# One exponential for two like score blocks, and TensorE's sums placed by steps of scores, in an attention kernel

## Chip, cores and metric

One Trainium2 chip, one core. The metric is the device time of the whole kernel in microseconds (us). PE is TensorE, ACT is ScalarE, DVE is VectorE, POOL is GpSimd, SP is the engine that issues the DMAs.

## What is computed

The input `x` has 2048 rows of 128 numbers, all float32. The reference is four residual blocks one after the other:

```
x = x + attention_a(layernorm(x))     # 16 heads of 8, causal, bias slope_h * (k - q)
x = x + ffn(layernorm(x))             # token shift, sigmoid gate, squared relu
x = x + attention_b(layernorm(x))     # linear attention with rotary positions
x = x + ffn(layernorm(x))
```

Only the softmax attention of the first block is touched by the change. For each head, `attn = Q K^T / sqrt(8) + bias`, with -inf where the key lies behind the query, then a softmax over the keys and a product with `V`.

## The kernel before

The heads are handled in transposed form: a block of scores has 128 keys on the partitions and up to 512 queries in the free dimension. The 2048 queries are four chunks `c` of 512, the 16 heads four groups `g` of 4, and a group is two pairs `u` of two heads `v`. The two heads of a pair sit on the two halves of TensorE's rows (64 each, `SIDE`), so their two score products run side by side, into two neighbouring banks of PSUM.

A block `(kb, w0, w1)` is key tile `kb` against the columns `w0` to `w1` of the chunk: the columns that the causal mask leaves, and only as far as the bias lets a head reach (`live`). A pair of heads has a list of blocks for a chunk (`pair_blocks`): blocks on the diagonal, which are 512, 384, 256 and 128 columns wide, take turns with blocks before it, which are mostly 512 wide. For the heads with steep slopes (g = 0, and pair 0 of g = 1) the blocks away from the diagonal are shorter and fewer, so one pair can have a block where the other has none.

A *unit* is the i-th block of both pairs of a group, 152 units in all, listed in `plan` in the order `ORDER` of (c, g). A *step* is what one exponential handles: before, one block of one pair, both heads, so up to 2 x 512 = 1024 columns; a unit has one or two steps, 296 in all.

- TensorE computes the scores of step n into the banks 2 * (n % 3) and the next one (`score`, the matmul is L1139). It waits for `exp_done`, until the exponential of step n - 3 is finished.
- ScalarE computes one exponential a step from PSUM into a slot in SBUF (`exps`, L532). There are four slots, used in turn by units: the first exponential of unit n also waits for `pv_done`, until the sums of unit n - 4 are done.
- VectorE masks the diagonal square of the units on the diagonal (`follow`, L856), and when a group has ended turns the sums (L790) and divides (`scale`).
- TensorE multiplies the probabilities with the values (`weigh`, the matmul is L1168): four matmuls for the four heads of a unit (eight records in the trace), which write four groups of 32 partitions and run side by side. They accumulate over the units of a group in bank 6 or 7 (`lane`). `weigh` waits for the unit's exponentials and its mask.

The order on TensorE is written out: while unit m is at hand, it issues the scores of pair 0 of unit m + 2, then `weigh` of unit m - 1, then the scores of pair 1 of unit m + 2. In the groups of chunk 3 some `aside`s of the next block (output projection, transposes of the second layernorm) stand behind that. After the last unit of `plan` the remaining sums are done and the rest of the kernel follows (72 us), which the change leaves alone.

The rows of queries and keys (`qr`, `kr`) are written by DMAs which SP issues from 9 to 115 us. SP also loads `x` again, once the sums of the last unit that used it as a slot are done.

Of the kernel before, what the change touches and what calls it, by code (L numbers as in the profile page):

```python
# [15 lines left out]
ACT = mybir.ActivationFunctionType  # L16
AX = mybir.AxisListType

P = 128
# [5 lines left out]
CH = 512  # L25
NCH = T // CH
TPC = CH // P
# [10 lines left out]
SIDE = 64  # L38
# [25 lines left out]
def program(nc, x_in, w_in, c_in, cb_in, krow_in, qrow_in, out):  # L64
    with ExitStack() as ctx:
        def sb(name, shape, dt):
            return ctx.enter_context(nc.sbuf_tensor(name, shape, dt))
# [4 lines left out]
        ps = ctx.enter_context(nc.psum_tensor("ps", [P, 8, CH], F32))  # L72
# [25 lines left out]
        summed = sb("summed", [P, 4 * TPC, V1], F32)  # L98
# [7 lines left out]
        with ExitStack() as rows:  # L106
# [3 lines left out]
            qr = [row_tensor(f"qr{n}") for n in range(NCH)]  # L110
            kr = [row_tensor(f"kr{n}") for n in range(NCH - 1)]
# [31 lines left out]
        def sems(names):  # L143
# [27 lines left out]
        s_done, exp_done, mask_done, pv_done, ot_ready, o_recip, o_norm = sems(  # L171
            "s_done exp_done mask_done pv_done ot_ready o_recip o_norm")
# [39 lines left out]
        def units_of(group, lane):  # L212
            c, g = group
            both = list(zip_longest(*(pair_blocks(c, 2 * g + u) for u in range(2))))
            return [(c, g, i, lane, i == len(both) - 1, blocks) for i, blocks in enumerate(both)]

        plan = []
        for k, group in enumerate(ORDER):
            units = units_of(group, k % 2)
            for c, g, i, lane, last, blocks in units:  # L220
                diagonal = all(b and b[0] >= TPC * c for b in blocks)
                steps_before, masks_before = (plan[-1].step + sum(b is not None for b in plan[-1].blocks),
                                              plan[-1].masks + plan[-1].masked) if plan else (0, 0)
                plan.append(Unit(c, g, i, lane, len(plan), last, blocks, diagonal, steps_before, masks_before))

        ends = [unit for unit in plan if unit.last]
# [6 lines left out]
        ASIDES = 3  # L233
        assert all(ends[k].i > i for k, i in ASIDE)
        assert all(b.n - a.n >= SCALE for a, b in zip(ends, ends[1:]))
        STEPS = plan[-1].step + sum(b is not None for b in plan[-1].blocks)

        def step_of(unit, u):
            return unit.step + (u if unit.blocks[0] else 0)

        def steps_with(unit):
            return unit.step + sum(b is not None for b in unit.blocks)


        def in_x(unit):
# [232 lines left out]
        def _(act):  # L478
# [37 lines left out]
            def exps(unit):  # L516
                slot = probs_slot(unit)
                act.wait_ge(pv_done, unit.n + 1)
                if unit.n == 3:

                    act.wait_ge(v_psum, NCH)
                if unit.n == min(other.n for other in plan if other.n % 4 == 1 and not in_x(other)):
                    for m in range(2):
                        for g in range(G):
                            act.wait_ge(rows_loaded[NCH - 1][m][g], ROW_LOADS[NCH - 1])
                for u, block in enumerate(unit.blocks):
                    if block:
                        _, w0, w1 = block
                        n = step_of(unit, u)
                        act.wait_ge(s_done, n + 1)  # L530
                        b = 2 * (n % 3)
                        nc.scalar.activation(slot[:, 2 * u:2 * u + 2, w0:w1], ps[:, b:b + 2, w0:w1], ACT.Exp).then_inc(exp_done, 1)  # L532
# [452 lines left out]
        def _(pe):  # L985
# [143 lines left out]
            def score(unit, u):  # L1129
                if unit is None or unit.blocks[u] is None:  # L1130
                    return
                kb, w0, w1 = unit.blocks[u]
                n = step_of(unit, u)
                wait_rows(unit.c, 0, unit.g)
                wait_rows(kb // TPC, 1, unit.g)
                pe.wait_ge(exp_done, n + 1)
                for v in range(2):
                    a, j = SIDE * v, 2 * unit.g + u
                    ins = nc.tensor.matmul(ps[:, 2 * (n % 3) + v, w0:w1],  # L1139
                                           kr[kb // TPC][a:a + SIDE, j, P * (kb % TPC):P * (kb % TPC + 1)],  # L1140
                                           qr[unit.c][a:a + SIDE, j, w0:w1], start=True, stop=True)
                ins.then_inc(s_done, 1)


# [5 lines left out]
            def weigh(unit):  # L1150
                if unit.i == 0:

                    ended = [place[e.c, e.g] for e in ends if e.lane == unit.lane and e.n < unit.n]
                    if ended:
                        pe.wait_ge(ot_ready, 1 + max(ended))
                    if place[unit.c, unit.g] == 1:

                        pe.wait_ge(v_ready[0], 2)
                        pe.wait_ge(v_ready[1], 2)
                    wait_asides(place[unit.c, unit.g] - 1)  # L1160
                pe.wait_ge(exp_done, 3 + steps_with(unit))
                if unit.masked:
                    pe.wait_ge(mask_done, unit.masks + 1)
                for v in range(4):
                    if unit.blocks[v // 2]:
                        kb, w0, w1 = unit.blocks[v // 2]
                        h = 4 * unit.g + v
                        ins = nc.tensor.matmul(ps[32 * v:32 * v + V1, 6 + unit.lane, w0:w1], vaug[:, kb, V1 * h:V1 * (h + 1)],  # L1168
                                               probs_slot(unit)[:, v, w0:w1],
                                               start=(unit.i == 0), stop=unit.last, skip_group_check=True)  # L1170
                ins.then_inc(pv_done, 1)
# [99 lines left out]
            def usual_path():  # L1271
                rows_seen.clear()
                pe.wait_ge(v_ready[0], 1)
                pe.wait_ge(v_ready[1], 1)
                nc.tensor.matmul(ps[:, 1, 0:2 * P], cb[:, B_ID:B_ID + P], cb[:, 0:2 * P], start=True, stop=True).then_inc(branched, 1)
                for u in range(2):
                    score(plan[0], u)

                pe.wait_ge(parts_ready, 2 * NCH)
                values(2)  # L1280
                for u in range(2):
                    score(plan[1], u)
                values(3)

                for unit, ahead in zip_longest(plan, plan[2:]):
                    score(ahead, 0)
                    if unit.n:
                        weigh(plan[unit.n - 1])
                    score(ahead, 1)
                    aside(unit)  # L1290
                weigh(plan[-1])

                mix_k_in(0, 0)
                mix_r_in(0, 0)
                project(3)
                mix_out(0, 0)
                mix_k_in(0, 1)
                mix_r_in(0, 1)
                mix_k_in(0, 2)
                mix_out(0, 1)  # L1300
                mix_r_in(0, 2)
                turn_ln2(3)
                mix_out(0, 2)
                mix_k_in(0, 3)
                turn_ln3(0)
                mix_r_in(0, 3)
                turn_ln3(1)
                mix_out(0, 3)
                k_b(0)
                v_b(0)  # L1310
                turn_ln3(2)
                k_b(1)
                q_b(0)
                v_b(1)
                k_b(2)
                turn_ln3(3)
                q_b(1)
                k_b(3)
                summarize(0)
                v_b(2)  # L1320
                v_b(3)
                q_b(2)
                summarize(1)
                q_b(3)
                summarize(2)
                summarize(3)
                turn_q(0)
                turn_q(1)
                numerators(0)
                turn_q(2)  # L1330
                numerators(1)
                turn_heads(0)
                numerators(2)
                project_b(0)
                turn_q(3)
                turn_heads(1)
                numerators(3)
                turn_heads(2)
                project_b(1)
                project_b(2)  # L1340
                turn_heads(3)
                turn_ln4(0)
                project_b(3)
                mix_k_in(1, 0)
                turn_ln4(1)
                mix_r_in(1, 0)
                turn_ln4(2)
                mix_k_in(1, 1)
                mix_r_in(1, 1)
                turn_ln4(3)  # L1350
                mix_k_in(1, 2)
                mix_r_in(1, 2)
                mix_out(1, 0)
                mix_out(1, 1)
                mix_k_in(1, 3)
                mix_out(1, 2)
                mix_r_in(1, 3)
                mix_out(1, 3)
# [72 lines left out]
```

## Time and profile before

| | us |
|---|---|
| Time of three runs, median (lowest to highest) | 333.89 (333.45 to 337.83) |
| The profiled execution: its own time | 333.41 |
| The profiled execution: span in the trace | 331.6 |
| TensorE busy in the span | 302.4 (91%) |
| ScalarE busy | 286.5 (86%) |
| VectorE busy | 162.2 (49%) |
| Mean granted clock of TensorE | 0.998 of full |

The first of the 296 exponentials begins at 24.2 us, the last ends at 259.4, and the last sum ends at 260.5; the attention of the first block is this stretch. A row of a timeline is a run of like instructions: its start, its length, the engine, the line, what is written from what, the shape of the first, how many. What stands in brackets is how long the engine was idle before it, and who ended that. Two instructions of one engine can overlap in such rows, since an instruction's record begins before the one ahead of it has drained; the cost of one in a stream is therefore read from the distance between two starts or two ends.

### The profile page before, as it was taken

The numbers are of one execution on the slowest core, as the hardware profiler recorded it, in microseconds if no ns is written. First come the engines' busy times: TensorE is split into PE (matmuls) and PEld (weight loads), VectorE is DVE, ScalarE is ACT, GpSimd is POOL, SyncE is SP. The second block draws the span as 40 slices with busy tenths as digits, with TensorE's granted clock in tenths as the row PEclk, the third lists the DMA queues.
The fourth block names the chain that finished last, engine by engine and source line by source line (L and its number), as shares of the span: only waits on it lengthen the run. The fifth ranks groups of instructions, "written<-read, shape, count | busy, mean of one in ns | idle before, by whom it ended". The sixth has DMA issues, their size and how long they took to land.

```text
span 331.6 us, 6146 instructions
## 1 busy us (share of the span) xinstructions
PE 302.4 (91%) x2306; PEld 131.1 (40%) x2306; DVE 162.2 (49%) x426; ACT 286.5 (86%) x410; POOL 57.5 (17%) x56
## 2 busy tenths in 40 slices
PE   2977999999999999999999999999999998979784
PEld 1633232333333222232323323333232567878563
DVE  6853243276633040311351461353713396999885
ACT  8548999989999999999899999998999488963782
POOL 5897000000040000000000110100000052811540
PEclk9999999999999999999999999999999999999999
DMA  7444443444464400000030000000000000000004
GB/s 212 118 114 98 103 140 96 104 110 88 108 199 104 103 2 0 2 0 2 0 112 17 2 1 2 0 2 0 2 1 2 0 3 0 3 0 2 0 0 131
DMA packets 14291, 16.45 MB, mean 50 GB/s; under 512 B 2513, under 2 KB 9041, under 8 KB 14161
## 3 DMA queue, kind: packets, MB, share of 16 engines
q1 hardware_dynamic: 14256, 16.01, 18.7%
q8 instruction: 20, 0.33, 0.4%
q14 instruction: 15, 0.11, 0.1%
HBM read 6.56 MB, written 2.62 MB: 28 GB/s over the span
## 4 chain that ended last, share of the span: by engine, by line
ACT 34%; PE 32%; DVE 16%; issue 13%; DMA 2%; POOL 1%; SPq 1%; DVEq 0%; ACTq 0%
ACT probs L532 23%; PE ps L1168 14%; PE ps L1139 10%; ACT x L532 8%; PE ps L993 4%; DVE stats L657 2%; ACT parts_last L532 2%; PE ps L1006 2%; DVE scr L916 2%; DMA x<-in_x 2%; DVE scr L905 1%; ACT scr L541 1%; POOL rstd L424 1%; DVE x L891 1%; DVE scr L930 1%
## 5 line engine op out<-in xcount | busy, mean ns | idle before, releaser
L532 ACT ACTIVATE probs<-ps 128x1024 f32<-128x1024 f32 (+5 forms) x223 | 169.0, 860 | 9.2 <-PE ps L1139 8.1
L1139 PE MATMUL ps<-qr,kr 64*128 64x512 f32 (+6 forms) x592 | 108.6, 420 | 7.2 <-ACT probs L532 4.2
L1168 PE MATMUL ps<-probs,vaug 128*9 128x512 f32 (+5 forms) x892 | 97.5, 495 | 1.1 <-DVE probs L856 1.1
L1139 PEld LDWEIGHTS ps<-qr,kr 64*128 64x128 f32 x592 | 49.3, 184 | 122.6 <-ACT probs L532 80.2
L856 DVE TENSOR_TENSOR probs<-probs,cs 128x512 f32<-128x512 f32 x60 | 41.3, 689 | 97.3 <-ACT probs L532 97.1
L424 POOL TENSOR_TENSOR rstd<-veps,neghalf 128x4 f32<-128x4 f32 x16 | 17.1, 1066 | 194.5 <-DVE veps L663 194.5
L532 ACT ACTIVATE x<-ps 128x1024 f32<-128x1024 f32 (+6 forms) x47 | 41.7, 950 | 0.1
L993 PE MATMUL ps<-w,scr 128*128 128x128 f32 x288 | 37.1, 280 | 2.6 <-DVE scr L877 1.1
L993 PEld LDWEIGHTS ps<-w,scr 128*128 128x128 f32 x288 | 34.4, 192 | 7.9 <-DVE scr L877 2.4
L532 ACT ACTIVATE parts_last<-ps 128x1024 f32<-128x1024 f32 (+5 forms) x26 | 24.1, 965 | 2.7 <-PE ps L1139 2.5
L1168 PEld LDWEIGHTS ps<-probs,vaug 128*9 128x9 f32 x892 | 13.7, 89 | 28.4 <-issue 16.4
L1168 PE MATMUL ps<-x,vaug 128*9 128x512 f32 (+6 forms) x188 | 22.8, 536 | 0.0
L790 DVE STREAM_TRANSPOSE ot<-ps 128x512 f32<-128x512 f32 x16 | 11.5, 717 | 16.7 <-PE ps L1168 16.4
L541 ACT ACTIVATE scr<-x,shift_by,rstd 128x128 f32<-128x128 f32 x36 | 14.8, 483 | 5.0 <-POOL shift_by L429 4.9
L988 PE MATMUL ps<-cs,scr 128*128 128x128 f32 x80 | 12.4, 280 | 2.6 <-ACT scr L541 2.1
L657 DVE BATCH_NORM_STATS2 stats<-x 128x6 f32<-128x128 f32 x64 | 13.9, 280 | 1.6 <-DMA x<-in_x 1.2
L488 ACT COPY scr<-ps 128x512 f32<-128x512 f32 x17 | 9.7, 579 | 5.8 <-PE ps L988 5.6
L453 POOL MEMSET kr<- 128x4096 f32 x1 | 3.5, 3514 | 61.1 <-DMA kr<-parts_mid 61.1
L1168 PE MATMUL ps<-parts_last,vaug 128*9 128x512 f32 (+5 forms) x104 | 13.9, 555 | 0.0
L988 PEld LDWEIGHTS ps<-cs,scr 128*128 128x128 f32 x80 | 8.8, 141 | 6.1 <-ACT scr L541 4.4
L815 DVE TENSOR_TENSOR x<-ps,x 128x512 f32<-128x512 f32 x4 | 2.8, 692 | 16.2 <-PE ps L993 16.2
L448 POOL MEMSET qr<- 128x4096 f32 x3 | 10.5, 3510 | 0.0
(106 smaller groups left out, 236.5 us busy)
## 6 DMA issues: line engine op xcount, KB each, us to landing
x<-in_x SPq DMA_DIRECT2D x8, 256.0 KB, 3.9
qr<-parts_mid SPq DMA_DIRECT2D x32, 64.0 KB, 2.5
kr<-parts_mid SPq DMA_DIRECT2D x32, 64.0 KB, 2.5
kr<-att SPq DMA_DIRECT2D x16, 64.0 KB, 2.4
qr<-att SPq DMA_DIRECT2D x16, 64.0 KB, 2.6
qr<-parts_last SPq DMA_DIRECT2D x16, 64.0 KB, 2.6
kr<-parts_last SPq DMA_DIRECT2D x16, 64.0 KB, 2.4
out_y<-x SPq DMA_DIRECT2D x4, 256.0 KB, 3.1
```

The costliest lines, as they stand in the source:

```text
L424: nc.gpsimd.tensor_tensor(rstd[:, n], veps[:, n], neghalf[:], ALU.pow).then_inc(ln_rstd[l], 1)
L448: nc.gpsimd.memset(z.bitcast(F32)[:, :, :], 0.0).then_inc(zeroed, 1)
L488: nc.scalar.copy(dst, ps[:, bank, :]).then_inc(ready, 1)
L532: nc.scalar.activation(slot[:, 2 * u:2 * u + 2, w0:w1], ps[:, b:b + 2, w0:w1], ACT.Exp).then_inc(exp_done, 1)
L541: ins = nc.scalar.activation(xh[:, P * t:P * (t + 1)], x[:, t, :], ACT.Identity, bias=shift_by[:, n, j:j + 1], scale=rstd[:, n, j:j + 1])
L657: nc.vector.bn_stats(stats[:, n, j, :], x[:, TPC * n + j, :]).then_inc(dve_step, 1)
L790: nc.vector.transpose(ot[:], ps[:, 6 + ends[k].lane, :]).then_inc(ot_ready, 1)
L856: nc.vector.tensor_tensor(slot, slot, cs[:, C_TRI:C_TRI + P].unsqueeze(1).broadcast_to([P, 4, P]), ALU.min).then_inc(mask_done, 1)
L988: ins = nc.tensor.transpose(ps[:, bank, P * j:P * (j + 1)], src[:, P * j:P * (j + 1)], ident)
L993: ins = nc.tensor.matmul(ps[:, bank, P * j:P * (j + 1)], src[:, P * j:P * (j + 1)], w[:, c0:c0 + D], start=True, stop=True)
L1139: ins = nc.tensor.matmul(ps[:, 2 * (n % 3) + v, w0:w1], kr[kb // TPC][a:a + SIDE, j, P * (kb % TPC):P * (kb % TPC + 1)], qr[unit.c][a:a + ...
L1168: ins = nc.tensor.matmul(ps[32 * v:32 * v + V1, 6 + unit.lane, w0:w1], vaug[:, kb, V1 * h:V1 * (h + 1)], probs_slot(unit)[:, v, w0:w1], st ...
```

## The change

Where both pairs of a unit have the same block and it is at most 256 columns wide, the unit is now one step: TensorE writes four score products, pair 0 into the columns from 0 and pair 1 into the columns from 256 of the same two banks, and ScalarE takes both with one exponential of four pieces (pair, head, columns) where there were two exponentials. `weigh` for such a unit is unchanged. The order on TensorE is no longer "pair 0, sum, pair 1" but goes by steps: the sum of unit n is issued right behind the scores of step `due[n]`, which is four steps after the unit's last one, or the first step of unit n + 4 if that comes sooner. The last four sums stand behind all scores.

```diff
+        def in_one(unit):
+            return unit.blocks[0] == unit.blocks[1] and unit.blocks[0][2] - unit.blocks[0][1] <= CH // 2
+
+        def steps_with(unit):
+            return unit.step + (1 if in_one(unit) else sum(b is not None for b in unit.blocks))
...
+        def has_step(unit, u):
+            return unit is not None and unit.blocks[u] is not None and not (u and in_one(unit))
 
         def step_of(unit, u):
-            return unit.step + (u if unit.blocks[0] else 0)
+            return unit.step + (u if unit.blocks[0] and not in_one(unit) else 0)
...
+                if in_one(unit):
+                    _, w0, w1 = unit.blocks[0]
+                    act.wait_ge(s_done, unit.step + 1)
+                    b = 2 * (unit.step % 3)
+                    nc.scalar.activation(slot[:, :, w0:w1].rearrange("p (u v) q -> p u v q", u=2),
+                                         ps[:, b:b + 2, :].rearrange("p v (u q) -> p u v q", u=2)[:, :, :, 0:w1 - w0],
+                                         ACT.Exp).then_inc(exp_done, 1)
+                    return
...
+                one = in_one(unit)
+                if one and u:
+                    return
...
-                for v in range(2):
-                    a, j = SIDE * v, 2 * unit.g + u
-                    ins = nc.tensor.matmul(ps[:, 2 * (n % 3) + v, w0:w1],
-                                           kr[kb // TPC][a:a + SIDE, j, P * (kb % TPC):P * (kb % TPC + 1)],
-                                           qr[unit.c][a:a + SIDE, j, w0:w1], start=True, stop=True)
+                for pair in range(2) if one else (u,):
+                    c0 = CH // 2 * pair if one else w0
+                    for v in range(2):
+                        a, j = SIDE * v, 2 * unit.g + pair
+                        ins = nc.tensor.matmul(ps[:, 2 * (n % 3) + v, c0:c0 + w1 - w0],
+                                               kr[kb // TPC][a:a + SIDE, j, P * (kb % TPC):P * (kb % TPC + 1)],
+                                               qr[unit.c][a:a + SIDE, j, w0:w1], start=True, stop=True)
...
+                due = [min(steps_with(unit) + 4, plan[unit.n + 4].step) for unit in plan[:-4]]
+                summed = 0
                 for unit, ahead in zip_longest(plan, plan[2:]):
-                    score(ahead, 0)
-                    if unit.n:
-                        weigh(plan[unit.n - 1])
-                    score(ahead, 1)
+                    for u in range(2):
+                        if has_step(ahead, u):
+                            score(ahead, u)
+                            while summed < len(due) and due[summed] <= step_of(ahead, u):
+                                weigh(plan[summed])
+                                summed += 1
                     aside(unit)
-                weigh(plan[-1])
+                for unit in plan[summed:]:
+                    weigh(unit)
```

Of the 152 units, 32 become one step: in each of the 16 groups the diagonal block of 256 columns and that of 128. The steps fall from 296 to 264.

## Rows read from the trace of the kernel before

**Rows 1.** The page: busy time by engine, its share of the span, instructions.

```profile
PE 302.4 (91%) x2306; PEld 131.1 (40%) x2306; DVE 162.2 (49%) x426; ACT 286.5 (86%) x410; POOL 57.5 (17%) x56
```

**Rows 2.** The page's costliest groups: busy, mean of one, idle before and its releaser.

```profile
L532 ACT ACTIVATE probs<-ps 128x1024 f32<-128x1024 f32 (+5 forms) x223 | 169.0, 860 | 9.2 <-PE ps L1139 8.1
...
L856 DVE TENSOR_TENSOR probs<-probs,cs 128x512 f32<-128x512 f32 x60 | 41.3, 689 | 97.3 <-ACT probs L532 97.1
...
L532 ACT ACTIVATE parts_last<-ps 128x1024 f32<-128x1024 f32 (+5 forms) x26 | 24.1, 965 | 2.7 <-PE ps L1139 2.5
```

**Rows 3.** Timeline of ACT, four stretches with one exponential each: two pairs of neighbours.

```profile
161.49 0.38 ACT L532 ACTIVATE probs<-ps 128x256 f32<-128x256 f32 x1
...
161.75 0.39 ACT L532 ACTIVATE probs<-ps 128x256 f32<-128x256 f32 x1
...
164.73 1.02 ACT L532 ACTIVATE x<-ps 128x1024 f32<-128x1024 f32 x1
...
165.63 1.03 ACT L532 ACTIVATE probs<-ps 128x1024 f32<-128x1024 f32 x1
```

**Rows 4.** Timeline of PE in chunk 2, around wide blocks (units 66 to 70).

```profile
127.00 0.73 PE L1139 MATMUL ps<-qr,kr 64*128 64x512 f32 x4
127.66 0.41 PE L1168 MATMUL ps<-probs,vaug 128*9 128x128 f32 x8
...
128.81 0.50 PE L1139 MATMUL ps<-qr,kr 64*128 64x512 f32 x2 [0.31 <-ACT probs L532]
129.24 1.05 PE L1168 MATMUL ps<-probs,vaug 128*9 128x512 f32 x8
130.22 0.93 PE L1139 MATMUL ps<-qr,kr 64*128 64x512 f32 x4
```

**Rows 5.** The chain that ended last, in order of time: first exponentials of groups (2, 2), (2, 3).

```profile
115.30 1.14 ACT probs L532
...
134.95 1.14 ACT probs L532
```

**Rows 6.** Timeline of ACT in the groups of chunk 0.

```profile
73.10 2.50 ACT L532 ACTIVATE probs<-ps 128x256 f32<-128x256 f32 x3 [0.40 <-PE ps L1139]
...
78.67 2.50 ACT L532 ACTIVATE probs<-ps 128x256 f32<-128x256 f32 x3 [0.40 <-PE ps L1139]
```

**Rows 7.** Timeline of PE in the same groups.

```profile
77.06 0.33 PE L1139 MATMUL ps<-qr,kr 64*128 64x128 f32 x2 [0.32 <-ACT x L532]
77.32 1.05 PE L1168 MATMUL ps<-probs,vaug 128*9 128x512 f32 x8
78.30 0.61 PE L1139 MATMUL ps<-qr,kr 64*128 64x128 f32 x4
```

**Rows 8.** Timeline of ACT in group (2, 0), units 86 to 92.

```profile
157.62 2.73 ACT L532 ACTIVATE probs<-ps 128x768 f32<-128x768 f32 x5 [0.48 <-PE ps L1139]
...
162.71 0.84 ACT L532 ACTIVATE probs<-ps 128x800 f32<-128x800 f32 x1 [0.57 <-PE ps L1139]
163.81 1.02 ACT L532 ACTIVATE probs<-ps 128x1024 f32<-128x1024 f32 x1 [0.26 <-PE ps L1139]
```

**Rows 9.** Timeline of PE in the same stretch.

```profile
162.54 0.73 PE L1168 MATMUL ps<-x,vaug 128*9 128x328 f32 x8
163.20 0.50 PE L1139 MATMUL ps<-qr,kr 64*128 64x512 f32 x2
```

**Rows 10.** Timeline of ACT at the end of group (3, 1), unit 109.

```profile
191.48 1.02 ACT L532 ACTIVATE parts_last<-ps 128x1024 f32<-128x1024 f32 x1 [0.95 <-PE ps L1139]
```

**Rows 11.** Timeline of PE at the end of the attention.

```profile
257.19 0.49 PE L1139 MATMUL ps<-qr,kr 64*128 64x512 f32 x2
...
258.48 2.02 PE L1168 MATMUL ps<-probs,vaug 128*9 128x512 f32 x16
```

**Rows 12.** Groups of ACT from 0 to 30 us: other patterns and the shortest activation.

```profile
L501 ACT COPY vaug<-ps 128x512 f32<-128x512 f32 x1 | 0.6, 587 | 0.3 <-PE ps L993 0.3
L481 ACT ACTIVATE warm<-neghalf 128x1 f32<-128x1 f32 x1 | 0.2, 202 | 0.0
```

More of the change, by code:

```diff
@@ L221, in program @@
                 diagonal = all(b and b[0] >= TPC * c for b in blocks)
-                steps_before, masks_before = (plan[-1].step + sum(b is not None for b in plan[-1].blocks),
-                                              plan[-1].masks + plan[-1].masked) if plan else (0, 0)
+                steps_before, masks_before = (steps_with(plan[-1]), plan[-1].masks + plan[-1].masked) if plan else (0, 0)
                 plan.append(Unit(c, g, i, lane, len(plan), last, blocks, diagonal, steps_before, masks_before))
@@ L235, in program @@
         assert all(b.n - a.n >= SCALE for a, b in zip(ends, ends[1:]))
-        STEPS = plan[-1].step + sum(b is not None for b in plan[-1].blocks)
+        STEPS = steps_with(plan[-1])
+        def has_step(unit, u):
+            return unit is not None and unit.blocks[u] is not None and not (u and in_one(unit))
         def step_of(unit, u):
-            return unit.step + (u if unit.blocks[0] else 0)
-        def steps_with(unit):
-            return unit.step + sum(b is not None for b in unit.blocks)
+            return unit.step + (u if unit.blocks[0] and not in_one(unit) else 0)
         def in_x(unit):
```

## Prediction

> **What bounds the kernel now.** I read the page first, then the list of groups, then the timelines of ScalarE and TensorE side by side. The page alone misleads. TensorE looks busier than ScalarE, 91% against 86% [rows 1]; but matmul records overlap, so I take costs from starts and ends.
>
> ScalarE: neighbouring exponentials of 256 columns end at 161.87 and 162.14 (start plus length), 0.27 apart; of 1024 at 165.75 and 166.66, 0.91 apart [rows 3]. The difference, 0.64 for 768 columns, is 0.833 ns a column, and 0.27 - 256 x 0.000833 leaves 0.06 us fixed. The other widths follow: 0.49 for 512, 0.70 for 768. So a full unit of two wide blocks costs ScalarE 1.82 us.
>
> TensorE: two score steps of 512 columns that need not wait take 0.66 together, 0.33 each; one that was waited for takes 0.43 (128.81 to 129.24); the sum of a full unit 0.98 (129.24 to 130.22), that of a 128-wide unit some 0.34 (a record of 0.41 less the 0.07 by which that of the wide sum, 1.05, overlaps what follows) [rows 4]. A full unit costs TensorE 1.64. With wide blocks ScalarE is the bound and TensorE has 0.18 a unit to catch up with. The 296 steps have 240,300 columns: 296 x 0.06 + 240,300 x 0.000833 = 218 us of work for ScalarE, in the 235 us from the first start to the last end. So about 17 us are ScalarE's idle time, and 12 of them stand in the list as idle before L532, 10.6 ended by the scores L1139 [rows 2]. The change can win the fixed part of 32 exponentials, and some of these 17.
>
> Where the idle time sits: at narrow blocks and at units of one block. In chunk 0 a group has blocks of 512, 384, 256 and 128, and the same three exponentials come back 5.57 us later (73.10, 78.67) [rows 6]. ScalarE's work in such a group is 2 x (0.91 + 0.70 + 0.49 + 0.27) = 4.74, so 0.83 are idle. TensorE's row says why: the first 128-wide score goes out at 77.06, then a whole sum of 0.98 stands ahead of the second, at 78.30 [rows 7], while ScalarE has only the last 512 columns and 0.27 of work in hand. In group (2, 0) units 91 and 92 have one block, and each score has a sum ahead of it (162.54, 0.66 before the score of unit 92 at 163.20) [rows 9]; ScalarE idles 0.57 and 0.26 there [rows 8]. Group (3, 0) repeats it. The largest, 0.95, is before unit 109, one block behind two sums and a projection [rows 10].
>
> **The change, part by part.**
>
> *One exponential for two.* 32 times 0.06 is 1.9 us less work for ScalarE; the columns stay. This pays only where ScalarE is the bound, so I count it inside the groups below. The Trainium skill ("ScalarE: Activation LUTs", section "What ACT_TABLE_LOAD costs") says that an activation has 186 ns fixed with immediate operands and that neighbours overlap by about 93 ns, which leaves 93 ns for each one dropped, 3.0 us by that page for 32, 1.1 more than by the rows. The measurement decides.
>
> *The new pattern.* The exponential reads four pieces across two banks and jumps back to the first bank once. No exponential before does that. The nearest row on the low side is the copy of values, which writes 64 pieces of 8 and takes 587 ns for 512 columns, as ordinary ones do [rows 12]: extra 0. On the high side a one-column activation takes 202 ns [rows 12]; if each return to the first bank cost that, 32 x 0.20 = 6.4 us. I take 0, since the copy is the nearest in kind.
>
> *Four score products in a step.* The same products and weight loads as two steps; one wait less. The sum of TensorE's work is the same. But both pairs must be written before ScalarE starts, so a 256-wide unit is ready 0.22 later than its first half was. It is hidden while ScalarE has a wide exponential in hand (0.91).
>
> *Sums by steps.* Between wide units `due` gives the old order. Around the merged units a sum comes up to one unit later. That adds a wait: take units 63 to 67. Now the scores of step 67.0 are issued when the exponential of 65.0 is done (time 0), the sum of unit 63 stands behind them, and the first exponential of unit 67 needs that sum's slot. It is ready at 0.05 + 0.43 + 1.05 for the whole sum + about 0.1 for the signal = 1.63; ScalarE has 0.91 (65.1) and 0.49 (66) to do and, since neighbours overlap by 0.1, could start at 1.3. So a gap of about 0.35 arises in each group at the unit after the 128-wide one. Behind it wait all later exponentials on ScalarE, and TensorE's scores three steps on.
>
> Group by group:
> - Eight groups with c and g at least 1 (all but (3, 1)). Before: the 24 steps of (2, 2) are 21,504 columns, 19.35 of work, and took 19.65 (115.30 to 134.95) [rows 5], so 0.30 are idle. After: work less 0.12, idle 0.35. Sum 0, within 0.1.
> - Four groups of chunk 0. Work 4.62. The second 128-wide score is no more behind a sum, so the gap of 0.57 goes; the new wait of 0.35 stays. 4.62 + 0.35 = 5.0 against 5.57: 4 x 0.55 = 2.2 us won. TensorE's own work there, 8 score products of pairs and 4 sums, is 4.6 (a score 0.33 at 512 columns and, as I estimate from the 77.06 row, 0.16 at 128; a sum 0.98 and 0.34), so it just keeps up; if it doesn't, this term halves.
> - Three groups with g = 0. The scores of the single blocks now come before the sums that stood ahead. I leave about 0.15 of each gap: 0.57 + 0.26 become 0.3 in (2, 0) and (3, 0), with 0.12 for the merges 0.65 each, and (1, 0) has one such unit, 0.5. The gap of 0.48 before unit 86 [rows 8] stays, no merged unit is near. Together 1.8 won.
> - Group (3, 1): 0.95 at unit 109 becomes 0.4; its narrow units had some 0.6 of gaps, and its sums there are of short blocks, so the new wait is hidden. With the merges 1.3 won.
> - The end. Before, the sum of unit 148 stood ahead of the last scores (257.19); three sums followed, and the last began when the last exponential was done [rows 11]. Now four stand behind: 0.43 + 3 x 0.98 = 3.4 after the last scores begin, against an exponential that is done 2.7 later at best (three of 0.91). The last sum is 0.6 late, and the rest of the kernel waits for it: 0.6 lost.
>
> *At nothing.* Masks: 0.69 each [rows 2], in chunk 0 four in a group, 2.8 of 5.0 us; sums come later than before, so masks have more time. Without that cover each would stand on the path with up to 0.7. The divisions at a group's end shift by at most a sum. SP's queue moves nothing: rows are loaded by its own order, and its reload of `x` waits for the sum of unit 93, which is as late after its exponential as before, with 10 us to its first use.
>
> Sum: -2.2 - 1.8 - 1.3 + 0.6 = -4.7. Against the profiled execution's 333.41 this gives 328.7; the median of the runs is 0.5 higher, 329.2. I say 329.0.
>
> **The rivals.**
>
> 1. *TensorE doesn't get its lead back* (the new wait repeats, the old gaps stay). For it: in chunk 0 TensorE's work (4.6) and ScalarE's (4.62) are equal, and each waited-for score costs 0.1 more. Against it: in wide stretches it regains 0.18 a unit. Chunk 0 gives 1.1 instead of 2.2, the g = 0 groups 0.9 instead of 1.8, and six groups lose 0.1 each: -4.7 + 1.1 + 0.9 + 0.6 = -2.1, 331.5.
> 2. *More of the idle time goes*: the slack that ScalarE's early narrow work used is kept, and the chain of small delays that feeds on itself (0.48 at unit 86, gaps by the asides in chunk 3) shortens as well. Half of the 17 us is the most that I can name at such places: -8, 325.5.
> 3. *Slower: the four-piece exponential is dear.* Place: the 32 merged steps. Price: two restarts of 0.13 to 0.20 each, 0.26 to 0.4 a step, 8 to 13 us against 4.7 won: 337 to 342. It decides from 0.15 us a step on. Against it stands the copy with 64 pieces.
> 4. *It does not do what it says*: if the 32 merged steps saved nothing fixed because the instruction is split inside into its pieces, 1.9 us fall away, of which about half counted: 330.
>
> **How the numbers follow.** Forecast 50%; rival 1, 20%; rival 2, 12%; rival 3, 6%; rival 4, 12%. The forecast's own spread is 1.5 us, from the 0.15 left at a gap (0 to 0.3, eleven places) and the new wait (0.2 to 0.5 in twelve groups). The range from 325.9 to 332.6 holds the forecast, rivals 1 and 4 and the half of 2; it leaves out rival 3 and some of 2 and 1, under 20%. About 2% is what a measurement of this kernel can tell from no change: 6.7 us, so faster means under 327.2. That is rival 2 and a tail of the forecast, 17%; slower over 340.6 is the dear half of rival 3, 4%; within 2%, 79%.
>
> **What would show it.** The profile after should have 264 exponentials; neighbours of the merged forms should end 0.49 (512 columns) and 0.91 (1024) after the one before. The three like exponentials of chunk 0 should return after 5.0. ScalarE's idle time at units 91, 92, 109 should be 0.4 or less, and a gap of about 0.35, ended by the sums L1168 and not by scores, should stand before the unit behind each 128-wide one. The last scores should be followed by four sums, and the last sum should end about 4.4 after them. The stretch behind should last 72 us as before. I am wrong if the merged exponentials take longer than their columns, if the masks L856 release sums, or if TensorE's waits for exponentials vanish in chunk 0, which would mean that it has become the bound.

## Result and the profile after

| | before | after |
|---|---|---|
| Time, median of six runs each, us | 334.61 (333.45 to 337.83) | 329.95 (329.03 to 332.01) |
| Ratio, with its 95% interval | | 0.9865 (0.9829 to 0.9901) |
| The profiled execution: time, span | 333.41, 331.6 | 330.01, 328.2 |
| First exponential begins, last sum ends | 24.2, 260.5 | 23.9, 255.8 |
| That stretch | 236.3 | 232.0 |
| Behind it, to the end | 71.1 | 72.4 |

The change makes the kernel 1.35% faster, 4.7 us by the medians. The forecast was 329.0, from a gain of 4.7 us on the profiled execution of before. Between the two profiled executions the difference is 3.4: the first exponential begins 0.3 earlier and the attention is 4.3 shorter, but the rest behind it took 1.3 longer, 1.0 of it in a stretch with a lower clock (last section).

The page after, busy time and costliest groups of ScalarE:

```profile
PE 302.3 (92%) x2306; PEld 133.7 (41%) x2306; DVE 161.7 (49%) x426; ACT 283.2 (86%) x378; POOL 57.6 (18%) x56
...
L546 ACT ACTIVATE probs<-ps 128x1024 f32<-128x1024 f32 (+5 forms) x159 | 141.6, 996 | 9.0 <-PE ps L1158 5.7
...
L536 ACT ACTIVATE probs<-ps 128x1024 f32<-128x1024 f32 (+1 forms) x32 | 27.6, 881 | 0.0
```

Against [rows 1] ScalarE has 32 instructions fewer and 3.3 us less busy time. Line 536 is the merged exponential, 32 of them, none of which waited. L546 is what L532 was. Its idle time before `probs` is nearly what it was in [rows 2], 9.0 against 9.2, but it has another owner. The waits of ScalarE in the trace of after (waiting line, releaser, us in total, times, longest):

```profile
ACT probs L546 <- PE ps L1158: 5.7, 10, 1.5
...
ACT probs L546 <- PE ps L1187: 2.6, 11, 0.4
```

Scores (L1158) release 5.7 us where they released 8.1 [rows 2]. New are 11 waits of up to 0.4 for sums (L1187), and two more ahead of `parts_last`: the slot of four units back.

Timelines of ScalarE and then of TensorE around units 64 to 67 of group (2, 2), after:

```profile
117.87 1.23 ACT L536 ACTIVATE probs<-ps 128x1024 f32<-128x1024 f32 x1
118.78 2.16 ACT L546 ACTIVATE x<-ps 128x1024 f32<-128x1024 f32 x2
120.58 0.84 ACT L536 ACTIVATE probs<-ps 128x512 f32<-128x512 f32 x1
121.61 1.94 ACT L546 ACTIVATE probs<-ps 128x1024 f32<-128x1024 f32 x2 [0.19 <-PE ps L1187]
```

```profile
119.47 0.44 PE L1158 MATMUL ps<-qr,kr 64*128 64x128 f32 x4
120.07 0.50 PE L1158 MATMUL ps<-qr,kr 64*128 64x512 f32 x2 [0.16 <-ACT x L546]
120.50 1.05 PE L1187 MATMUL ps<-probs,vaug 128*9 128x512 f32 x8
121.47 0.51 PE L1158 MATMUL ps<-qr,kr 64*128 64x512 f32 x2
```

This is the new wait as it was stepped out. The exponential of 65.0 ends and releases the scores of 67.0 at 120.07; 0.43 later the sum of unit 63 begins, takes 1.05 to its end at 121.55, and at 121.61 the first exponential of unit 67 can start. The one before it began at 120.58 and, with 512 columns, needed 0.48 to 0.49: the merged form ends at 121.42, the pair before it at 120.94. A stream would have gone on 0.1 before 121.42, so ScalarE lost about 0.3. The bracket says 0.19, since it counts from the end of a record.

The groups of chunk 0, ScalarE, after, to be compared with [rows 6]:

```profile
72.28 1.94 ACT L546 ACTIVATE probs<-ps 128x1024 f32<-128x1024 f32 x2 [0.28 <-PE ps L1187]
74.10 1.52 ACT L546 ACTIVATE x<-ps 128x768 f32<-128x768 f32 x2
75.48 1.55 ACT L536 ACTIVATE probs<-ps 128x1024 f32<-128x1024 f32 x2
77.31 1.03 ACT L546 ACTIVATE probs<-ps 128x1024 f32<-128x1024 f32 x1 [0.28 <-PE ps L1187]
```

The period was 5.57 and is 5.03. The gap in front of the second 128-wide exponential is gone, and the whole of what idles now is the wait for the sum. TensorE in the same groups, after, for [rows 7]:

```profile
70.17 1.06 PE L1158 MATMUL ps<-qr,kr 64*128 64x128 f32 x6
71.17 1.05 PE L1187 MATMUL ps<-probs,vaug 128*9 128x512 f32 x8
```

Its wait of 0.32 for an exponential no longer shows. A timeline prints idle time only from 0.15 on. The first row holds three pairs of scores, and the third pair, 512 columns of the next group, starts at 70.74, 0.13 after the pair ahead of it has ended.

Group (2, 0), ScalarE, after, for [rows 8]:

```profile
154.21 1.75 ACT L546 ACTIVATE probs<-ps 128x768 f32<-128x768 f32 x3 [0.48 <-PE ps L1158]
155.88 1.02 ACT L536 ACTIVATE probs<-ps 128x1024 f32<-128x1024 f32 x1
156.80 1.23 ACT L546 ACTIVATE x<-ps 128x656 f32<-128x656 f32 x2
157.90 0.62 ACT L536 ACTIVATE probs<-ps 128x512 f32<-128x512 f32 x1
158.54 1.99 ACT L546 ACTIVATE probs<-ps 128x800 f32<-128x800 f32 x2
```

The idle 0.57 and 0.26 before units 91 and 92 no longer show; the 0.48 before unit 86 stands as it stood. Group (3, 1), ScalarE, after, where [rows 10] had 0.95:

```profile
165.89 0.81 ACT L546 ACTIVATE probs<-ps 128x768 f32<-128x768 f32 x1 [0.47 <-PE ps L1158]
...
171.49 0.87 ACT L546 ACTIVATE parts_last<-ps 128x832 f32<-128x832 f32 x1 [0.23 <-PE ps L1187]
...
186.53 1.03 ACT L546 ACTIVATE parts_last<-ps 128x1024 f32<-128x1024 f32 x1
187.94 1.94 ACT L546 ACTIVATE probs<-ps 128x1024 f32<-128x1024 f32 x2 [0.38 <-PE ps L1158]
```

Unit 109 (186.53) comes without a gap, but 0.38 of it has moved to the unit behind, 0.23 stands in front of unit 101 for a sum, and 0.47 before the second exponential of unit 96.

The end of the attention, TensorE, after, for [rows 11]:

```profile
251.78 0.50 PE L1158 MATMUL ps<-qr,kr 64*128 64x512 f32 x2 [0.42 <-ACT probs L546]
252.21 1.05 PE L1187 MATMUL ps<-probs,vaug 128*9 128x512 f32 x8
253.07 1.04 PE L1187 MATMUL ps<-parts_last,vaug 128*9 128x512 f32 x8
253.93 1.90 PE L1187 MATMUL ps<-probs,vaug 128*9 128x512 f32 x16
```

Four sums behind the last scores. They start 0.86 apart, not 0.98: a sum that follows a sum needs 0.12 less than one with a score behind it.

### The profile page after: what moved, and what is told of

It is laid out like the page before. It is cut to its first block, busy times and chain, and to the rows that moved or that the text cites. A ratio compares the mean times of both kernels' runs of the same rounds, so it can differ in the third digit from the quotient of the medians.

```text
span 328.2 us, 6114 instructions
## 1 busy us (share of the span) xinstructions
PE 302.3 (92%) x2306; PEld 133.7 (41%) x2306; DVE 161.7 (49%) x426; ACT 283.2 (86%) x378; POOL 57.6 (18%) x56
## 4 chain that ended last, share of the span: by engine, by line
PE 47%; ACT 26%; DVE 16%; issue 8%; POOL 1%; DMA 1%; DVEq 0%; POOLq 0%
PE ps L1187 22%; ACT probs L546 16%; PE ps L1158 16%; ACT x L546 5%; PE ps L1007 4%; DVE stats L671 2%; PE ps L1020 2%; ACT parts_last L546 2%; DVE scr L930 2%; DVE scr L919 1%; POOL rstd L430 1%; PE ps L1002 1%; ACT scr L555 1%; DMA x<-in_x 1%; DVE x L905 1%
## 5 line engine op out<-in xcount | busy, mean ns | idle before, releaser
L546 ACT ACTIVATE probs<-ps 128x1024 f32<-128x1024 f32 (+5 forms) x159 | 141.6, 996 | 9.0 <-PE ps L1158 5.7
L1158 PE MATMUL ps<-qr,kr 64*128 64x512 f32 (+6 forms) x592 | 107.8, 418 | 4.4 <-DMA kr<-parts_mid 1.5
L1158 PEld LDWEIGHTS ps<-qr,kr 64*128 64x128 f32 x592 | 50.2, 184 | 118.0 <-ACT probs L546 58.3
L1187 PE MATMUL ps<-probs,vaug 128*9 128x512 f32 (+5 forms) x892 | 97.4, 494 | 0.7 <-DVE probs L870 0.7
L870 DVE TENSOR_TENSOR probs<-probs,cs 128x512 f32<-128x512 f32 x60 | 41.0, 688 | 91.2 <-ACT probs L546 54.6
L546 ACT ACTIVATE x<-ps 128x1024 f32<-128x1024 f32 (+6 forms) x47 | 41.6, 976 | 0.1
L536 ACT ACTIVATE probs<-ps 128x1024 f32<-128x1024 f32 (+1 forms) x32 | 27.6, 881 | 0.0
L1187 PEld LDWEIGHTS ps<-probs,vaug 128*9 128x9 f32 x892 | 13.7, 88 | 28.8 <-issue 20.5
L546 ACT ACTIVATE parts_last<-ps 128x1024 f32<-128x1024 f32 (+5 forms) x26 | 23.9, 957 | 1.7 <-PE ps L1158 1.0
L1187 PE MATMUL ps<-x,vaug 128*9 128x512 f32 (+6 forms) x188 | 22.8, 535 | 0.0
L1187 PE MATMUL ps<-parts_last,vaug 128*9 128x512 f32 (+5 forms) x104 | 13.9, 555 | 0.0
```

What stands on the lines that cost most here:

```text
L536: nc.scalar.activation(slot[:, :, w0:w1].rearrange("p (u v) q -> p u v q", u=2), ps[:, b:b + 2, :].rearrange("p v (u q) -> p u v q", u=2)[ ...
L870: nc.vector.tensor_tensor(slot, slot, cs[:, C_TRI:C_TRI + P].unsqueeze(1).broadcast_to([P, 4, P]), ALU.min).then_inc(mask_done, 1)
L1158: ins = nc.tensor.matmul(ps[:, 2 * (n % 3) + v, c0:c0 + w1 - w0], kr[kb // TPC][a:a + SIDE, j, P * (kb % TPC):P * (kb % TPC + 1)], qr[unit ...
```

## Experiments

From the first exponential of group (1, 2) on, the groups' periods repeat between kernels to some hundredths. Group (1, 1) before it doesn't (13.1 to 15.4 us): in it rows still arrive, and in some executions the clock is low for 3.4 us. So the kernels are compared by the stretch from that exponential to the end of the last sum, in which the granted clock was full in all ten traces. Differences of 0.02 are rounding. Their expectations speak of the stretch from the very first exponential, 13.7 longer in the kernels before and after; the differences are what counts.

| kernel | median, us | ratio to before, timed beside it | stretch from group (1, 2) | against before |
|---|---|---|---|---|
| before | 334.61 | | 222.60 | |
| after | 329.95 | 0.9865 (0.9829 to 0.9901) | 218.30 | -4.30 |
| merging only | 331.07 | 0.9841 (0.9762 to 0.9919) | 218.14 | -4.46 |
| steps only | 333.96 | 0.9952 (0.9917 to 0.9987) | 221.80 | -0.80 |
| two exponentials in a merged step | 331.64 | 0.9896 (0.982 to 0.9972) | 218.89 | -3.71 |
| sums due after three steps | 327.30 | 0.9746 (0.9677 to 0.9815) | 214.90 | -7.70 |
| slot's sums one step sooner | 329.34 | 0.9773 (0.9704 to 0.9841) | 217.12 | -5.48 |
| pieces bank by bank | 331.18, one run | | 218.28 | -4.32 |
| sums due after five steps | 335.38, one run | | 223.91 | +1.31 |
| three steps, last sums mended | 327.20 | 0.9745 (0.9664 to 0.9825) | 214.04 | -8.56 |

Group by group, start of a group's first exponential to that of the next, us:

| kernel | (1, 2) | (0, 1) | (1, 0) | (2, 2) | (2, 0) | (3, 1) | (3, 3) |
|---|---|---|---|---|---|---|---|
| before | 12.31 | 5.57 | 10.44 | 19.65 | 11.93 | 26.77 | 27.75 |
| after | 12.28 | 5.03 | 9.38 | 19.61 | 11.26 | 26.42 | 27.83 |
| merging only | 12.38 | 4.92 | 10.01 | 19.41 | 11.60 | 26.72 | 27.45 |
| steps only | 12.32 | 5.56 | 10.05 | 19.65 | 11.30 | 26.82 | 28.14 |
| slot's sums one step sooner | 12.38 | 4.72 | 9.45 | 19.41 | 11.25 | 26.53 | 27.89 |
| due after three | 12.14 | 4.67 | 9.30 | 19.19 | 10.55 | 26.66 | 28.76 |
| due after five | 12.49 | 5.22 | 10.42 | 19.83 | 12.02 | 27.26 | 27.63 |

(The last column ends with the last exponential.)

**Merging only.** The old order on TensorE, `has_step` and `due` unused:

```diff
-                    for u in range(2):
-                        if has_step(ahead, u):
-                            score(ahead, u)
-                            while summed < len(due) and due[summed] <= step_of(ahead, u):
-                                weigh(plan[summed])
-                                summed += 1
+                    score(ahead, 0)
+                    if unit.n:
+                        weigh(plan[unit.n - 1])
+                    score(ahead, 1)
                     aside(unit)
```

> The merged steps alone, TensorE's order by units as before (score of pair 0, sum, score of pair 1). Measured by the stretch from the first exponential's start to the last sum's end: 236.3 us before, 232.0 with the whole change. My theory: the merging itself wins most, both its fixed cost (1.9 us) and the sum that no longer stands between two narrow scores, so 232.5 (between 232.0 and 233.0); the gap of 0.35 behind the 128-wide unit is absent and gaps at units of one block (0.57, 0.26, 0.95) are still there. Rival, that the order by steps is what wins: 234.4, the fixed cost alone.

Measured 231.8 for that stretch, 0.2 under the range; 218.14 from group (1, 2): the merging gives all of it, and slightly more than the whole change. ScalarE's rows around units 91 and 92 show what it leaves:

```profile
161.00 0.84 ACT L546 ACTIVATE probs<-ps 128x800 f32<-128x800 f32 x1 [0.37 <-PE ps L1158]
162.09 1.03 ACT L546 ACTIVATE probs<-ps 128x1024 f32<-128x1024 f32 x1 [0.26 <-PE ps L1158]
```

0.57 has become 0.37, the 0.26 is as it was, and so is the 0.95 before unit 109. In chunk 0 the period is 4.92, shorter than the whole change's 5.03, and in (2, 2) 19.41 against 19.61: these groups have no wait for a sum.

**Steps only.** `in_one` answers no to everything:

```diff
-            return unit.blocks[0] == unit.blocks[1] and unit.blocks[0][2] - unit.blocks[0][1] <= CH // 2
+            return False
```

> The sums placed by steps alone, nothing merged, 296 exponentials. Same stretch. My theory: only the units of one block gain (six of them, about 0.3 to 0.6 each) and group (3, 1), and the 0.57 gap before the second 128-wide exponential in chunk 0 stays, less 0.25 at the end for the fourth sum: 235.3 (234.8 to 235.8). Rival, that the order is what wins: 233.5 or less.

Measured 235.6, and 0.80 less than before from group (1, 2) on. All of the gain is in the three groups with g = 0 (10.05, 11.30, and 11.18 for (3, 0), 1.65 together); the other groups of chunk 3 and the end (0.25) give half of it back. Group (3, 1), where a gain was expected, has none: the 0.95 before unit 109 is gone, but 0.47 now stands before the second exponential of unit 96 and 0.38 before unit 110, both ended by scores. Chunk 0 has its old rows again, at another time:

```profile
73.64 2.49 ACT L546 ACTIVATE probs<-ps 128x256 f32<-128x256 f32 x3 [0.40 <-PE ps L1158]
```

The two parts alone win 4.46 and 0.80, together 4.30. The order alone is worth 1.65 at units of one block. Once steps are merged it costs 0.1 in three groups of chunk 0 and 0.2 in (2, 2), where sums now fall behind the first scores of the unit that wants their slot. The 0.4 that it costs in (3, 3) is something else: it is there without merging too (28.14 against 27.75), as 0.46 ahead of the second exponential of unit 138, ended by scores.

**Two exponentials in a merged step.**

```diff
-                    nc.scalar.activation(slot[:, :, w0:w1].rearrange("p (u v) q -> p u v q", u=2),
-                                         ps[:, b:b + 2, :].rearrange("p v (u q) -> p u v q", u=2)[:, :, :, 0:w1 - w0],
-                                         ACT.Exp).then_inc(exp_done, 1)
+                    for u in range(2):
+                        ins = nc.scalar.activation(slot[:, 2 * u:2 * u + 2, w0:w1],
+                                                   ps[:, b:b + 2, CH // 2 * u:CH // 2 * u + w1 - w0], ACT.Exp)
+                    ins.then_inc(exp_done, 1)
```

> The whole change, but a merged step is taken by two exponentials (pair 0, pair 1) behind one wait, with one signal at the end. Scores and sums as in the changed kernel. Prices the fixed part by itself. From the rows: 32 x 0.06 = 1.9 us more than the changed kernel, less where ScalarE has idle time anyway: 233.5 (233.0 to 234.0) for the stretch. By 93 ns for each one dropped, as the Trainium skill gives: 235.0. If the four-piece pattern were itself dear, this would be no slower than the change: 232.0.

Measured 232.0 for the whole stretch, and 0.59 more than after from group (1, 2) on (group (1, 1) happened to be 0.54 shorter, which alone brings the whole to the 232.0 that a dear pattern would have given). The 1.9 missed. The groups say where it stays: 0.06 more in each group with c of 1 or more (except (3, 1), none), that is, one of the two merges of a group, and nothing in chunk 0. The other merge lies between the release of the scores of unit n + 4 and the sum that they hold up: ScalarE waits there in either case, and a shorter exponential only lengthens the wait. The ends of the exponentials show it: the first one of unit 67 ends 1.15 after the one before it where after has 1.21, and the first of a group of chunk 0 ends 1.18 after where after has 1.30, so one or both fixed parts come off the wait. So 0.59 us of the 4.3 are the fixed part of an instruction. The other 3.7 remain when the exponential is split again, so they belong to the steps and their order. That it is both pairs' scores in a row with no sum between, and a ring of three steps that reaches further ahead, is how I read it; no run has the one without the other. (The Trainium skill, "ScalarE: Activation LUTs", section "What ACT_TABLE_LOAD costs", has 186 ns fixed and an overlap of about 93 ns between neighbours. The estimate from it, 93 ns for each activation dropped, would have been 3.0 us; the trace does not agree, with 0.06 an instruction.)

**Pieces bank by bank.** The same exponential, `"p (u v) q -> p v u q"` on both sides, so that PSUM is read without going back:

> The whole change, the merged exponential reads and writes its four pieces head by head, so that PSUM is read bank by bank, never going back, and SBUF is written out of order. Prices the jump back between banks. My theory: a piece costs nothing, neighbours of the merged forms end 0.49 and 0.92 after the one before as now, stretch 232.0. Rival, that the jump costs: each merged exponential gets shorter by 0.05 or more.

218.28 against 218.30, and groups like (2, 2) with 19.61 in both. The merged forms end 0.49 and 0.92 after the one before in either order of the pieces. The jump between banks costs nothing, and neither does the scattered side. This takes away the ground of the slower rival.

**Sums due after three steps.**

```diff
-                due = [min(steps_with(unit) + 4, plan[unit.n + 4].step) for unit in plan[:-4]]
+                due = [min(steps_with(unit) + 3, plan[unit.n + 4].step) for unit in plan[:-4]]
```

> The whole change, but a sum is due three steps after its unit's last one instead of four. If the gap of 0.35 to 0.55 that stands in nearly every group before the unit behind the 128-wide one comes from the slot's wait on the sum four units back, then it goes here: 12 gaps, 229.5 for the stretch against 232.0 (229 to 230.5). Rival, that TensorE is short of time there in any order: 232.0, no change. Third, sums wait for masks when they come a step sooner: over 232.5 with idle time of TensorE ended by masks L870.

Measured 229.4, the whole of it, although group (1, 1) was 0.8 longer in that execution: 3.4 less than after from group (1, 2) on, where 2.5 were expected. All waits of ScalarE for sums are gone. That the number met the first theory's is partly luck, as the next run shows: only about a third of the 3.4 is the slot's wait. ScalarE in chunk 0 has no gap left beyond 0.1, with a period of 4.65 to 4.67, its work being 4.62:

```profile
71.44 1.55 ACT L536 ACTIVATE probs<-ps 128x1024 f32<-128x1024 f32 x2
72.91 1.94 ACT L546 ACTIVATE probs<-ps 128x1024 f32<-128x1024 f32 x2
74.73 1.52 ACT L546 ACTIVATE x<-ps 128x768 f32<-128x768 f32 x2
76.11 1.55 ACT L536 ACTIVATE probs<-ps 128x1024 f32<-128x1024 f32 x2
```

Group (3, 3) got 0.9 longer than after's. There the sum of unit 136 stands ready while its mask waits on VectorE behind a mix of the next block. TensorE's row:

```profile
229.74 1.05 PE L1187 MATMUL ps<-probs,vaug 128*9 128x512 f32 x8 [0.65 <-DVE probs L870]
```

So the third theory of that run holds too, at this one place: the scores of unit 139 stand behind that sum, and ScalarE idles 0.79 before them.

**Slot's sums one step sooner.** Only the date set by the slot is moved, which sends 30 of the sums out one step sooner:

```diff
-                due = [min(steps_with(unit) + 4, plan[unit.n + 4].step) for unit in plan[:-4]]
+                due = [min(steps_with(unit) + 4, plan[unit.n + 4].step - 1) for unit in plan[:-4]]
```

> The whole change, but where the slot of unit n + 4 sets the date, the sum of unit n goes out one step sooner, before the first scores of unit n + 4 and not behind them; else nothing moves. Only the new wait is touched. My theory: the gap before the unit behind the 128-wide one (0.45 to 0.55 between starts, 12 places, ended by the sums) falls to 0.1 to 0.2: the stretch from the first exponential to the last sum is 229.5 to 230.5 after 232.0. Rival, that the gap is TensorE's lack of time and only changes its place: 232.0, the idle time now ended by scores. If the changed spot alone explains all that the due of three steps won, this equals its 229.4.

230.9 for the whole stretch and 217.12 from group (1, 2), 1.18 less than after; the expected 1.5 to 2.5 was too much. ScalarE has no wait for a sum left. (2, 2) goes at 19.41, as with the merging alone, and chunk 0 at 4.72, where the merging alone had 4.92. So the new wait cost 0.2 in four wide groups and 0.3 in three of chunk 0, and not the 0.3 to 0.35 each that its own gap shows: without it a part of the gap comes back in front of the scores. Of these 1.7 us 0.5 go again in other groups, so that 1.2 are left. Three steps win 2.2 more than this: 0.70 in (2, 0), 0.90 in (3, 0), 0.51 in (0, 0) and 0.2 to 0.3 in (1, 2), (1, 3) and (2, 2), with 0.86 lost in (3, 3). ScalarE waits for no sum in either kernel, so this is not the slot's wait. That there the sum goes out while TensorE would else wait for a bank of scores is how I read it; no run separates it.

**Sums due after five steps.** The same line with `+ 5`.

> The whole change, but a sum is due five steps after its unit's last instead of four, the slot's date as it is. If the wait for the slot is what late sums cost, nearly every unit now has it, since the date is then set by the slot almost everywhere: the exponentials wait for sums, the stretch grows by 0.1 to 0.35 in each of about 110 wide units, some 5 to 25 us more, 237 to 257, ScalarE's idle time ended by the sums L1187. Rival, that only the total of TensorE's work counts: 232 to 233.

237.7 for the whole stretch. From group (1, 2) 223.91: 5.6 more than after, slower than before by 1.3 us in this stretch. The list of ScalarE's groups from 40 to 250 us:

```profile
L546 ACT ACTIVATE probs<-ps 128x1024 f32<-128x1024 f32 (+5 forms) x141 | 124.3, 988 | 8.0 <-PE ps L1187 6.4 <-PE ps L1158 1.2
```

6.4 us of this are now ended by sums. It is the low end of what was expected, and the expectation had miscounted the dates: where every unit has two steps, five steps after a unit's last still come one step before the first of unit n + 4, so the slot sets the date at only 30 of the units. The wait stays where it was, once or twice in most groups and up to four times where g = 0, and gets longer (0.41 before unit 67, 0.19 in after). That the order of the same work moves the stretch from 214.9 (three) to 218.3 (four) to 223.9 (five) is the clearest sign that TensorE's total does not set these times.

**Three steps, last sums mended.** A version that was to beat both:

```diff
-                due = [min(steps_with(unit) + 4, plan[unit.n + 4].step) for unit in plan[:-4]]
+                due = [min(steps_with(unit) + (4 if (unit.c, unit.g) == (3, 3) else 3),
+                           plan[unit.n + 4].step if unit.n + 4 < len(plan) else STEPS - 2) for unit in plan[:-3]]
```

> A version meant to be better: sums due three steps after their unit, four in the last group (where masks stand behind a mix of the next block on VectorE), and only the last three sums behind all scores. My theory: 229.4 with three steps everywhere, the last group's 1.0 comes back but for 0.2, and the last sum ends 0.25 sooner: stretch 228.3 (227.8 to 228.9), 2.9% under the kernel before by the runs' times. Rival, that the waits for masks are not what the last group lost: 229.2.

229.5 for the whole stretch, above the range, because group (1, 1) took 15.4 us in that execution with its clock low from 29.7 us; from group (1, 2) on 214.04, 0.86 less than three steps alone. Group (3, 3) came to 28.17 (28.76 with three steps, 27.83 after): the 0.79 before unit 139 is gone, since its scores now go ahead of the sum that waits for its mask (0.41 still), but 0.30 before unit 137, which three steps brought and after doesn't have, stays. And the last sum ends 1.10 after the last exponential, as before the change, instead of 1.35. The runs do not tell it from three steps alone (327.20 and 327.30); both are 2.5% under before, where 2.9% were expected, and about twice the gain of the change.

## Why the prediction held, step by step

- **The sum** was -4.7 against the profiled execution. The attention measured -4.3. The sign, the size and most places were right; the terms that were off go both ways (0.9 and 0.4 less won, 0.6 more won and 0.35 less lost than forecast) and nearly cancel by luck. That the medians differ by the same 4.7 is luck too: they include falls of the clock (last section), and the spans of after's own runs lie 3 us apart.
- **The cost of an exponential.** The merged forms end 0.48 to 0.49 and 0.92 after the one before, as the columns and 0.06 say. Right. That the pattern costs nothing: right, shown bank by bank. But the 1.9 us were counted nearly everywhere as a gain and are worth 0.59. The working set ScalarE's "work less 0.12, idle 0.35" in each wide group; in truth the idle time is what is left over when TensorE's chain sets the date. It went unnoticed, as the sum for these groups came out right (0 forecast, between -0.05 and +0.13 measured in each).
- **Chunk 0**, -2.2: measured -1.78 (5.57 to 5.03 in three groups, 0.17 in the first). The mechanism as described: the gap of 0.57 gone, the wait for the sum in its place.
- **The new wait**: right in place, releaser and size (0.3 to 0.35). Thirteen of them show as waits, the one in (3, 1) too. What it costs is less, 1.2 us in all.
- **Groups with g = 0**, -1.8: measured -2.41, of which steps alone win 1.65. The merging alone wins 1.08 there as well. Least was known here, and 0.15 left at each gap was too careful in (1, 0).
- **Group (3, 1)**, -1.3: measured -0.35. This is the term that failed. "Its sums there are of short blocks, so the new wait is hidden" was wrong: 0.23 stands before unit 101, ended by L1187. And the order by steps doesn't only win there: of the 0.95 at unit 109 it moved 0.38 to unit 110, and it put 0.47 before unit 96. Both stand at the same places with the order alone, whose group (3, 1) takes 26.82 against 26.77.
- **The end**, 0.6 lost: 0.25 measured. Sums in a row cost 0.86, not 0.98; the overlap of a score with the sum ahead of it had been taken for a part of the sum. Three times 0.12 is the difference.
- **The rest** was to last as before. Behind the last sum it is 71.1 before and 71.2 to 71.5 in four of the later kernels; the 72.4 of after's profile has a cause of its own, below.
- **The signs of being wrong.** Sums wait for masks (L870) once in after, 0.7, and twice before, 1.1 together: no more than they did. TensorE's wait for an exponential in chunk 0 nearly vanished, from 0.32 to 0.13, which was to mean that it had become the bound. It hadn't: the same work goes through at 4.65 to 4.67 a group instead of 5.03 when its sums come a step sooner. There TensorE's rows have no gap either, so that its work, forecast at 4.6, does "just keep up".
- **The rivals.** TensorE did get its lead back. The dear pattern is excluded; of its price of 0.13 to 0.20 for a restart the lower end had no row. The one that nothing fixed would be saved came near for a reason that it didn't give: the saving is real, and mostly lands in idle time.

What the forecast did not see is how the two parts of the change stand to each other. It credited the order by steps with the gains at units of one block and the merging with the rest, which the single parts bear out in the main (0.80 and 4.46). It did not see that the order's new wait uses up its gain: on top of the merging, the order without that wait is worth 1.0 (218.14 to 217.12), and the wait costs 1.2 (217.12 to 218.30).

## What to carry to other kernels

Where two engines hand work to and fro through a short ring, cost a change by the chain that sets the next date, not by either engine's instructions: here a fixed 0.06 dropped 32 times was worth a third of its face value, while moving the sums one step up in the queue was worth 3.4 us over the kernel. When steps change their size, derive all dates in the queue again, from both ends (the result is ready; the buffer is wanted), and try one step sooner and later: three orders of identical work lay 9 us apart. And try a change's parts alone, since a part can be used up by the other.

## What was not expected of the hardware

The clock that is granted to TensorE falls for 3.4 us at a time to the lower of its two levels (1.2 GHz), in some executions and not in others: in seven of the ten profiled ones it begins at 24 to 30 us, in five at 291 to 298. (In all ten it is low once more in the last 2 us.) Windows of the kernel after (columns: stretch; length; busy time of PE, PEld, DVE, ACT, POOL with instructions; granted clock; DMA):

```profile
275.00:290.00 15.00, 14.41 (x122) 13.63 (x121) 14.93 (x37) 11.77 (x24) 9.57 (x8) 1.00 0.01 2
290.00:305.00 15.00, 12.45 (x88) 11.57 (x86) 12.80 (x37) 6.96 (x14) 1.22 (x2) 0.89 0.01 1
```

TensorE had been busy 14.41 of 15 us before the fall. The same work before the change, aligned by the last sum, ran at full clock, here too behind 14.41 busy:

```profile
279.70:294.70 15.00, 14.41 (x122) 13.62 (x121) 14.93 (x37) 11.76 (x24) 9.57 (x8) 1.00 0.01 2
294.70:309.70 15.00, 11.84 (x95) 10.70 (x94) 13.80 (x44) 7.73 (x16) 1.55 (x3) 1.00 0.00 1
```

Counted from the last sum, like instructions of ScalarE and VectorE are at the same time in both to 0.02 us ahead of the dip, and 1.0 us later in after behind it. The five profiled executions that have this fall take 72.1 to 72.5 us behind the last sum, the five without it 71.1 to 71.5. The executions of after have spans from 327.2 (clock 0.999) to 330.2 (0.989), so these falls make much of the spread between its runs, and a gain of 1% is better read from a stretch of the trace that has none. What brings such a fall about stays open: no run here was made for it.
